# The opening of an attention and expert layer: first rows in four transfers of one tile, two of four tiles scaled on GpSimd

## The reference

```python
x = x + attention(layernorm(x), w_q, w_k, w_v, w_o)      # 32 heads of 16
x = x + experts(layernorm(x), gate_w, w1, w2, w3)        # 8 experts, top 2, silu(h1) * h3
def _layernorm(x, axis=-1, eps=1e-05):
    m = jnp.mean(x, axis=axis, keepdims=True)
    v = jnp.var(x, axis=axis, keepdims=True)
    return (x - m) / jnp.sqrt(v + eps)
```

## Time and profile before

| | us |
|---|---|
| median of three runs | 556.28 |
| lowest and highest | 556.05, 557.72 |
| profiled execution: time | 556.68 |
| profiled execution: span | 554.9 |

### The profile page before, as it was taken

How to read it: one execution, slowest core, us unless ns; L and a number is a source line. 1 busy time by engine, 2 the same in 40 slices (tenths; PEclk the granted TensorE clock), 3 DMA queues, 4 the chain that set the end, 5 groups by cost and what they waited for, 6 DMA issues and landing times.

```text
span 554.9 us, 9691 instructions
## 1 busy us (share of the span) xinstructions
PE 535.2 (96%) x3504; PEld 390.2 (70%) x3504; DVE 386.5 (70%) x706; ACT 324.6 (58%) x480; POOL 115.3 (21%) x145
## 2 busy tenths in 40 slices
PE   8999999999999999999999999999999999999991
PEld 6887665333333333333777989999999999999980
DVE  6915657999998999961879986745738284667650
ACT  5322115777778777878355464746566475757540
POOL 4300111002012021622001220333342321241202
PEclk9999999999999999999999999999999999999997
DMA  8390367676475753004464599684845757585112
GB/s 322 114 114 1 56 104 88 80 89 77 80 99 73 91 71 99 12 22 164 161 241 146 184 338 331 160 295 65 319 108 194 237 156 263 136 298 158 27 25 38
DMA packets 29069, 78.19 MB, mean 141 GB/s; under 512 B 7645, under 2 KB 8925, under 8 KB 24539
## 3 DMA queue, kind: packets, MB, share of 16 engines
q1 hardware_dynamic: 23722, 68.84, 46.9%
q0 software_dynamic: 5296, 8.69, 8.2%
HBM read 53.11 MB, written 9.32 MB: 113 GB/s over the span
## 4 chain that ended last, share of the span: by engine, by line
PE 79%; DVE 12%; issue 3%; DMA 2%; ACT 2%; POOL 1%; SPq 0%; POOLq 0%; DVEq 0%; ACTq 0%
PE ps L725 16%; PE ps L726 15%; PE ps L727 15%; PE ps_o L737 8%; DVE neg_max L1464 8%; PE ps L756 6%; PE ps L768 4%; PE ps_m L756 3%; PE ps L796 2%; PE ps_o L725 1%; PE ps_m L725 1%; PE ps_m L1019 1%; PE ps_o L726 1%; PE ps_o L727 1%; PE ps_m L726 1%
## 5 line engine op out<-in xcount | busy, mean ns | idle before, releaser
L1247 ACT ACTIVATE probs_t<-ps 128x1024 f32<-128x1024 f32 x128 | 124.2, 1022 | 31.4 <-PE ps L768 30.7
L1464 DVE TENSOR_REDUCE neg_max<-ps 128x1 f32<-128x512 f32 x170 | 111.3, 684 | 12.1 <-PE ps L756 9.9
L725 PE MATMUL ps<-xgT_hi,w_hi 128*128 128x256 f32 (+7 forms) x380 | 109.5, 288 | 0.1
L726 PE MATMUL ps<-xgT_lo,w_hi 128*128 128x256 f32 (+7 forms) x380 | 108.5, 286 | 0.0
L727 PE MATMUL ps<-xgT_hi,w_lo 128*128 128x256 f32 (+7 forms) x380 | 108.5, 286 | 0.0
L725 PEld LDWEIGHTS ps<-xgT_hi,w_hi 128*128 128x128 f32 x380 | 72.0, 189 | 0.8 <-DVE xgT_lo L1724 0.6
L726 PEld LDWEIGHTS ps<-xgT_lo,w_hi 128*128 128x128 f32 x380 | 72.0, 189 | 0.1
L727 PEld LDWEIGHTS ps<-xgT_hi,w_lo 128*128 128x128 f32 x380 | 71.9, 189 | 0.0
L756 PE MATMUL ps<-k_stack,q_stack 48*128 48x512 f32 x170 | 68.6, 459 | 1.8 <-DVE neg_max L1464 0.4
L737 PE MATMUL ps_o<-probs_t,v_ones 128*32 128x512 f32 x512 | 68.1, 605 | 0.0
L1741 DVE TENSOR_TENSOR act<-gate,ps 128x256 f32<-128x256 f32 (+7 forms) x48 | 20.7, 430 | 65.6 <-PE ps L727 53.3
(11 more groups left out here) (327 smaller groups left out, 978.1 us busy)
## 6 DMA issues: line engine op xcount, KB each, us to landing
w_sb<-w SPq DMA_DIRECT2D x16, 1024.0 KB
w_sb<-w SPq DMA_DIRECT2D x8, 1536.0 KB
w_sb<-w SPq DMA_DIRECT2D x8, 1152.0 KB
q_stack<-q_hi SPq DMA_DIRECT2D x32, 128.0 KB, 4.9
k_stack<-k_hi SPq DMA_DIRECT2D x32, 128.0 KB, 4.7
q_stack<-q_lo SPq DMA_DIRECT2D x16, 128.0 KB, 4.5
k_stack<-k_lo SPq DMA_DIRECT2D x16, 128.0 KB, 5.9
q_hi<-o_raw SPq DMA_DIRECT2D x16, 128.0 KB, 5.2
```

Source lines behind the costliest of these rows:

```text
L725: pe.matmul(o, x_hi, w_hi, start=start, stop=False)
L726: pe.matmul(o, x_hi, w_lo, start=False, stop=False)
L1247: a.activation(probs_t[:, kc % 2, 2 * half:2 * half + 2, :], ps4[:, 2 * (n % 2):2 * (n % 2) + 2, :], ACT.Exp, scale=D ** -0.5).then_inc(s_ ...
L1464: v.tensor_reduce(neg_max[:, g % 2, col:col + 1], max_bank(g, u2), AX.X, ALU.max, negate=True).then_inc(s_mx, 1)
```

## The change

- SP issues x of batch 0 as four transfers of one tile. The first increments s_x[0], the others three semaphores of their own.
- VectorE waits for each tile ahead of its statistics (`statistics`). The order is: statistics of 0 and 1, variance of both, statistics of 2, reciprocal of 0 and 1 and scaling of tile 0, statistics of 3, variance of 2 and 3, reciprocal of both and scaling of tile 2.
- The reciprocal increments s_rstd. GpSimd waits for it and scales tile 1, and at its second increment tile 3, each incrementing s_xn_odd. Its wait ahead of v_ones is now for two increments of s_xn and two of s_xn_odd.
- TensorE waits for s_xn_odd ahead of the transposes of tiles 1 and 3 of batch 0; its counts of s_xn for the other tiles are adapted. Batch 1 is done as before, by VectorE alone.

```diff
-        s_x_more = sem("s_x_more")
+        s_x_more = [sem(f"s_x_more{t}") for t in range(1, TPB)]
+        s_rstd, s_xn_odd = sem("s_rstd"), sem("s_xn_odd")
...
-            for half, done in ((0, s_x[0]), (1, s_x_more)):
-                at = slice(half * TPB // 2, (half + 1) * TPB // 2)
-                sp.dma_start(x_sb[:, at, :], x_t[:, at, :]).then_inc(done, 16)
+            for t, done in enumerate((s_x[0], *s_x_more)):
+                sp.dma_start(x_sb[:, t, :], x_t[:, t, :]).then_inc(done, 16)
...
-            pool.wait_ge(s_xn, TPB)
+            for t in range(1, TPB, 2):
+                pool.wait_ge(s_rstd, t // 2 + 1)
+                pool.tensor_scalar(x_sb[:, t, :], x_sb[:, t, :], aggr[:, t, 0:1], rstd[:, t:t + 1],
+                                   ALU.subtract, ALU.mult).then_inc(s_xn_odd, 1)
+            pool.wait_ge(s_xn, TPB // 2)
+            pool.wait_ge(s_xn_odd, TPB // 2)
             pool.memset(v_ones[:, :, :, :, 1], 1.0).then_inc(s_const, 1)
...
-                    pe.wait_ge(s_xn, b * TPB + i + 1)
+                    if b == 0 and i % 2:
+                        pe.wait_ge(s_xn_odd, i // 2 + 1)
+                    else:
+                        pe.wait_ge(s_xn, i // 2 + 1 if b == 0 else TPB // 2 + i + 1)
...
-            v.wait_ge(s_x[0], 16)
-            spread(x_sb, 0, 2)
+            def statistics(t):
+
+                v.wait_ge((s_x[0], *s_x_more)[t], 16)
+                return v.bn_stats(stats[:, t, :], x_sb[:, t, :])
+
+            def scaled_even(t):
+
+                norms[0] += 1
+                v.wait_ge(s_std, norms[0])
+                v.reciprocal(rstd[:, t:t + 2], rstd[:, t:t + 2]).then_inc(s_rstd, 1)
+                v.wait_ge(s_rstd, norms[0])
+                v.tensor_scalar(x_sb[:, t, :], x_sb[:, t, :], aggr[:, t, 0:1], rstd[:, t:t + 1],
+                                ALU.subtract, ALU.mult).then_inc(s_xn, 1)
+
+            statistics(0)
+            link(statistics(1))
             variance(0, 2)
-            v.wait_ge(s_x_more, 16)
-            spread(x_sb, 2, TPB)
+            statistics(2)
+            scaled_even(0)
+            link(statistics(3))
             variance(2, TPB)
-            scaled(x_sb, x_sb, 0, 2, s_xn)
-            scaled(x_sb, x_sb, 2, TPB, s_xn)
+            scaled_even(2)
```

## The result

| | before | changed |
|---|---|---|
| median of 13 runs each, us | 556.25 | 559.48 |
| lowest, highest | 556.00, 560.35 | 557.98, 561.38 |
| profiled execution: time, span | 556.68, 554.9 | 558.35, 556.6 |

The ratio is 1.0042, 95% interval 1.0023 to 1.0062: the change makes the kernel slower by about 0.4%. The medians lie 3.2 us apart, which is 0.6%. 556.0 was forecast.

What follows compares the result with a forecast made beforehand. TensorE mostly bounds the kernel, through a chain from the first rows' transfer to q0 at 11.35. Fourth tile 9.54 plus 1.52 puts q0 at 11.06, 0.29 earlier: 556.28 - 0.29 = 556.0 us; range 555.0 to 557.5.

Steps and rivals of the forecast that it cites:

- VectorE's new order: Opening: statistics from 3.52, second epsilon at 7.55, tile 2 scaled by 8.74, 0.65 earlier than before.
- GpSimd's tile 3: Opening: GpSimd scales the fourth tile in 0.80 (ends 0.61 and 1.28), done at 9.54, 0.29 earlier than 9.83.
- only one of its inputs is wide: Reason for pricing GpSimd's scaling at 0.80, nearer the 0.61 row than the 1.28 row with two wide inputs.
- port wait of 0.54: GpSimd's tile 3, released at about 8.20, waits for VectorE's scaling of tile 2 and runs from 8.74.
- the prediction's own 1.52: Opening: time from the fourth tile scaled (9.83) to q0's first matmul (11.35).
- The port: Opening: VectorE and GpSimd share a port locked for a full instruction; GpSimd's scalings wait for VectorE's, 8.74 to 9.54 for tile 3.
- so it moves data faster: VectorE's scaling takes 0.55 against 0.69 for an equally wide subtraction, so it was taken to hold the port too.
- The transfers: Start: four one-tile transfers land at 3.50, 4.15, 4.80 and 5.46; two extra issues (0.92) push later loads at no cost.
- a rival with a chance of 0.07: Opening: wq's piece lands 0.92 later and holds the second root; q0 0.38 later, 556.7 us; chance 0.07.
- Nothing waits for a fixed hour: Behind the opening: no later wait absorbs a shift of q0, so the 0.29 gained goes to the end.
- GpSimd first: Opening: GpSimd takes the port ahead of VectorE in both pairs; q0 1.06 later, 557.3 us; chance 0.13.

Runs made afterwards that it cites:

- the second trace of the changed kernel: The changed kernel run again unedited, on the same chip as the kernel before: median 561.29 us, ratio 1.0069; q0 at 13.87 in its trace.
- The shift alone: The kernel before with 25 instead of 6 filler matmuls ahead of q0: ratio 1.0025, full-clock launches 558.6 us against 556.9.
- filling the gaps: The changed kernel with 8 and 14 filler matmuls ahead of the second and fourth tiles' transposes: median 559.2 us, ratio 1.0043.

## Why the prediction was wrong

The change is slower where no difference was forecast, and 559.48 lies above the range. By the prediction's steps:

- **VectorE's new order: right.** Each start within 0.05 in the profiled launch.
- **GpSimd's tile 3: the step that failed.** I took 0.80 with ends at 0.61 and 1.28. It costs 2.09 with VectorE's statistics alone beside it, and 2.35 and 2.74 in place. The upper end was the dearest row at hand, an operation with two wide inputs; "only one of its inputs is wide" made it look like an upper bound, and it was none. The fourth tile was scaled at 11.21 and not at 9.54, 1.67 later. By the terms, the price is 1.93 of it (2.73 for 0.80). The queue adds 0.28: the second scaling, released at about 8.2, could only start at 8.48 behind the first, where I had tile 1 done at 7.42. The port wait of 0.54 that I had added did not come and goes off. With the prediction's own 1.52 from there, q0 is at 12.73, 1.38 later; with the transfers as late as in the second trace of the changed kernel (scaled at 12.03) 2.2 later. The full-clock launches say 2.0.
- **The page's figure was no support for it.** The Trainium skill's "GPSIMD Engine Reference", section "Elementwise — side-by-side cycle accounting", gives about 0.77 for 512 elements in its best case, a tight loop. The same width took 2.09 here (a copy 0.61), so the figure's agreement with my 0.80 carried no evidence.
- **The port: half right, and minor.** GpSimd and VectorE do hold each other, by up to 0.4 (0.92 for 0.55) or 0.5 (2.59 for 2.09). Which one waited went both ways, and GpSimd's long scaling hardly held VectorE's (0.60 for 0.55 at 8.15, with the operation in flight until 8.47). Nor did it hold the subtraction for wq's piece, which I had waiting until 9.54: it ran at 8.68 and took 0.67, as before, with GpSimd's second scaling in flight. The step "so it moves data faster" was faulty as well: 0.55 is for one wide input, 0.69 for two. The rule of the Trainium skill's "SBUF — State Buffer", section "Terms", that the loser fully blocks, agrees with the product and the epsilon at 21.95 and not with these two rows. Why GpSimd's second scaling took 0.4 more than its first was not tested.
- **The transfers: right in the profiled launch, not in most.** Statistics at 3.5 came. But wq's piece, whose push I priced at nothing and whose later landing was a rival with a chance of 0.07, was copied after 7.1 in six of eight traces with four transfers, and the third tile, forecast to land at 4.80, came late enough for VectorE to wait in five of them, which the prediction had nowhere. The late landing isn't in the loss (two transfers with GpSimd's scalings lose 2.1), but it took the gain that the four transfers were to bring: 0.0 and 0.2 above before instead of 0.57 below.
- **TensorE's clock: not in the prediction.** By its sum TensorE never waited long for GpSimd, so a wait of 1.65 and what follows from it did not come up. The fall costs 0.97 at the end of q1 in the profiled launch. Beyond that the medians differ by the share of launches whose clock falls in the opening, the attention or among the experts.
- **"Nothing waits for a fixed hour": right.** The shift alone, 1.8 of q0, came out as 1.8 at the end. In the profiled launch of the changed kernel 1.7 of 2.35 arrived.

The "GpSimd first" rival had the right side by the wrong cause: VectorE's scalings were not held in the changed kernel. What stays open: why the share of launches with a fallen clock is 14 of 19 for the changed kernel, and why filling the gaps left it at 7 of 12. The waits in the opening are in both its traces and account for one stretch; the stretches later on occur in the kernel before too, more on one chip than on another. Why small first transfers land late is open too; no experiment reached into that. No version beat the kernel before beyond doubt.

## What to carry to other kernels

Measure an operation on the engine that is to do it before moving work there: a row of another form, even a seemingly heavier one, is no upper bound. When two pieces of work go to an idle engine in sequence, price the second with the first in front of it. A late operand can cost TensorE twice, by the wait and by its clock behind it (about 1.0 us here, on a wait of 1.65 that followed one of 1.07), so look at the granted clock behind every new wait.

## What the runs showed of the hardware

- On GpSimd a subtract and multiply of 128x512 in float32 takes 2.09 with per-partition operands and 1.93 with constants, one multiply 1.58, a product of two tiles 1.28, a copy 0.61, each with some VectorE work beside it. With VectorE idle, 128x256 takes 1.23. VectorE does the first in 0.55.
- While GpSimd scaled a tile, VectorE's scaling took 0.60 (0.56 in the kernel before) and its subtraction 0.67 (0.69 there). While GpSimd copied one, VectorE's scaling took 0.92.
- 40 equal filler matmuls at the start of the kernel ended between 7.0 and 8.6 in different launches with the granted clock shown as 1.00.
